# Graph-network kernel: the output pass opens with earlier guards, two tiles made ahead and eight undivided tiles

## The reference, cut to what matters

```python
hp = (node_adj > 0) @ hW              # hW = h @ W[k], per head k
hm = (node_adj < 0) @ hW
e_plus  = leaky_relu(concat([hp, hm], 1) @ a, 0.2)
e_minus = leaky_relu(concat([hm, hp], 1) @ a, 0.2)
att = where(edge_adj > 0, e_plus[None, :], NEG_INF)
att = where(edge_adj < 0, e_minus[None, :], att)
att = softmax(att, axis=1)
edge_support += (att * edge_adj) @ hW     # summed over the 3 heads, then / 3
...
node_output = gru_cell(edge_support, h, node weights)
x = x + de * edge_output + dn * node_output
```

## Time and profile before

| | |
|---|---|
| median of 3 runs | 2030.96 us |
| the profiled execution's own time | 2032.97 us |
| span of its trace (first to last instruction) | 2031.2 us |
| mean granted TensorE clock | 0.978 of full speed |
| PE / DVE / ACT busy | 92% / 74% / 67% of the span |
| sums pass, last part (1239 to 1306 us) | PE busy 66.80 of 67 us |
| output pass, first chunk (1306 to 1399 us) | PE busy 81.00 of 93 us, ACT 89.54 |
| output pass, third chunk's 88 us (1488 to 1576 us) | PE busy 86.13, ACT 77.92 |

### The profile page before, as it was taken

The page is one execution under the profiler, slowest core; times in us unless marked ns, Lnnn a source line. Parts: engine busy times, 40 slices in busy tenths (PEclk is TensorE's granted clock), DMA queues, the critical chain, the costliest instruction groups (busy, mean ns, idle before and its releaser), DMA issues.

```text
span 2031.2 us, 24901 instructions
## 1 busy us (share of the span) xinstructions
PE 1867.2 (92%) x9423; PEld 1309.6 (64%) x9423; DVE 1505.4 (74%) x2278; ACT 1366.1 (67%) x1760; POOL 13.4 (1%) x15
## 2 busy tenths in 40 slices
PE   4877889699988999999999989899999999999998
PEld 4877888488878989955555556544555555554554
DVE  6222226888877888887878753499898898988986
ACT  4222221466668999988777630399898898988984
POOL 0000000000010000000000000000000000000000
PEclk9999999899999999989999999999999999999999
DMA  9999997688866767669999789533343333334230
GB/s 382 424 424 424 424 425 279 238 323 314 318 250 221 270 243 265 249 219 361 354 327 363 265 311 373 178 119 114 114 154 116 114 119 117 132 123 146 99 99 21
DMA packets 88794, 498.12 MB, mean 245 GB/s; under 512 B 9265, under 2 KB 13362, under 8 KB 39266
## 3 DMA queue, kind: packets, MB, share of 16 engines
q1 hardware_dynamic: 84354, 494.34, 65.1%
q10 hardware_dynamic: 4320, 2.20, 0.4%
HBM read 456.55 MB, written 39.94 MB: 244 GB/s over the span
## 4 chain that ended last, share of the span: by engine, by line
PE 52%; DMA 15%; ACT 14%; DVE 14%; issue 5%; SPq 0%; ACTq 0%; DVEq 0%
PE bank L1972 15%; DMA work<-in_adj_rows 12%; PE bank L1946 4%; ACT work L755 4%; PE bank L1785 3%; ACT work L750 3%; PE bank L1787 3%; PE bank L1786 3%; PE bank L1858 2%; DVE work L1581 2%; PE bank L1980 2%; PE bank L1981 2%; ACT work L906 2%; PE bank L1979 2%; PE bank L1863 2%
## 5 line engine op out<-in xcount | busy, mean ns | idle before, releaser
L1972 PE MATMUL bank<-work,reg 128*128 128x512 f32 x760 | 359.2, 597 | 14.6 <-DVE ring L1532 7.9
L906 ACT ACTIVATE work<-x,e 128x512 f32<-128x512 f32 x552 | 355.1, 709 | 0.4 <-ACT linebuf L871 0.4
L1581 DVE TENSOR_TENSOR work<-work,ring 128x1536 f32<-128x1536 f32 x184 | 321.2, 1749 | 9.2 <-ACT work L906 9.0
L1696 PE MATMUL bank<-reg,ring 128*128 128x128 f32 x2048 | 251.0, 284 | 52.3 <-DMA ring<-in_adj_units 29.7
L1696 PEld LDWEIGHTS bank<-reg,ring 128*128 128x128 f32 x2048 | 243.4, 199 | 58.8 <-issue 37.7
L1816 PE MATMUL bank<-reg,ring 128*128 128x129 f32 x2048 | 242.8, 281 | 26.0 <-DVE ring L1275 25.7
L1816 PEld LDWEIGHTS bank<-reg,ring 128*128 128x128 f32 x2048 | 238.2, 197 | 29.9 <-DVE ring L1275 19.1
L1972 PEld LDWEIGHTS bank<-work,reg 128*128 128x128 f32 x760 | 142.6, 190 | 136.2 <-issue 112.0
L1979 PE MATMUL bank<-s_lo,h_hi 128*128 128x512 f32 x240 | 186.0, 775 | 4.9 <-DVE a_lo L1560 3.7
L1275 DVE SCALAR_TENSOR_TENSOR ring<-ring,work 128x2048 f32<-128x2048 f32 x64 | 147.2, 2300 | 39.3 <-ACT work L755 39.2
L1170 DVE TENSOR_TENSOR a_lo<-ring,a_hi 128x2048 fp32r<-128x2048 f32 x64 | 147.5, 2315 | 17.9 <-ACT a_hi L706 17.5
(11 more groups left out here) (295 smaller groups left out, 3073.7 us busy)
## 6 DMA issues: line engine op xcount, KB each, us to landing
ring<-in_adj_units SPq DMA_DIRECT2D x320, 1024.0 KB, 5.5
work<-in_adj_rows SPq DMA_DIRECT2D x38, 1024.0 KB, 22.6
ring<-masks SPq DMA_DIRECT2D x64, 512.0 KB, 5.7
ring<-in_adj_rows SPq DMA_DIRECT2D x26, 1024.0 KB, 22.4
masks<-work SPq DMA_DIRECT2D x48, 512.0 KB, 8.7
masks<-ring SPq DMA_DIRECT2D x16, 512.0 KB, 8.2
x<-lines SPq DMA_DIRECT2D x8, 768.0 KB, 10.4
ring<-lines SPq DMA_DIRECT2D x8, 768.0 KB, 7.9
```

Of the source, the lines that this page charges most:

```text
L906: last = act.activation(tiles(n)[:, k * W:(k + 1) * W], guard(c, k), ACT.Sigmoid, bias=e6[:, t * SCORES + k:t * SCORES + k + 1], scale=-1.0)
L1581: dve.tensor_tensor(tv, tv, spread(ring[:, ring_at("out", g, q * W, W)], HEADS, 1), ALU.mult).then_inc(s_y, 1)
L1696: last = pe.matmul(o, ring[:, first:first + P], reg1[:, t * P:(t + 1) * P], start=t == 0 and i == 0, stop=t == T - 1 and i == Q - 1)
L1972: return pe.matmul(bank[1 + k][:, :], reg1[:, t * P:(t + 1) * P], tiles(c * T + t)[:, k * W:(k + 1) * W], start=t == 0, stop=t == T - 1)
```

## The change

`WHOLE_TILES = 8` is new. The third head of tiles 0 to 7 is no longer divided: ACT makes no high part and DVE no low part for them, and PE multiplies all three heads in plain f32. The places of high parts are counted over the divided tiles alone (`cuts`). `weights(0)` and `weights(1)` move in ACT's list from behind `keep_norm(8)` to between `guards(7)` and `guard_rows(7)`. SP issues the fetch of the first guards before the mask load of unit 44 instead of behind that of unit 63.

```diff
+WHOLE_TILES = 8
...
         CUT = T - 2
+        cuts = [n for n in range(C * T) if n % T < CUT and n >= WHOLE_TILES]
+
+        def is_cut(n):
+
+            return n % T < CUT and n >= WHOLE_TILES
 
         def cut_index(n):
 
-            return (n // T) * CUT + n % T
+            return cuts.index(n)
...
                     sp.dma_start(xs_d, x[:, :]).then_inc(s_xs, 16)
+                if n == 44:
+                    load_guards(0)
                 load_masks(n)
-            load_guards(0)
             load_guards(1)
...
+            for c in range(1, C):
+                keep_norm(c)
+                guards(c)
+                if c == C - 1:
+                    for n in range(AHEAD):
+                        weights(n)
+                guard_rows(c)
+            keep_norm(C)
...
             def third_high(n):
 
                 i = cut_index(n)
                 if i >= PLACES:
-                    act.wait_ge(*tile_used(i - PLACES + 2 * ((i - PLACES) // CUT)))
+                    act.wait_ge(*tile_used(cuts[i - PLACES]))
...
-            for n in range(AHEAD):
-                weights(n)
             for c in range(C):
...
-                    if t < CUT:
+                    if is_cut(n):
                         third_high(n)
...
-                        if 0 < t <= CUT:
+                        if t and is_cut(n - 1):
                             third_low(n - 1)
...
-                            if k == LAST:
+                            if k == LAST and is_cut(c * T + t):
                                 pe.wait_ge(s_ylo, cut_index(c * T + t) + 1)
                                 last = third_tile(c, t)
                             else:
-                                head_tile(c, t, k)
+                                last = head_tile(c, t, k)
```

More of the change, by code:

```diff
@@ L873, in guard_rows @@
                 act.dma_start(lines_d[:, (c - 1) * W:c * W], linebuf[:, :]).then_inc(s_line, 16)
[L875 to L879, removed]
-            def keep_edge_support(c):
-                act.wait_ge(s_es, c)
-                if c > 1:
-                    act.wait_ge(s_gm["out"], c - 1)
-                act.activation(n_temps[0], bank[0][:, :], ACT.Copy, scale=1.0 / HEADS).then_inc(s_src["out"], 1)
-            def store(c):
-                act.wait_ge(s_res["out"], c)
-                act.dma_start(out_d.rearrange("(t p) f -> p t f", p=P)[:, at(c, Q, -Q, Q), :],
-                              res.rearrange("p (t f) -> p t f", f=P)).then_inc(s_store, 16)
             def weights(n):
@@ L908, in weights, with keep_edge_support, store @@
                 last.then_inc(s_exp, 1)
+            for c in range(1, C):
[6 more added lines that the diff above has]
+            keep_norm(C)
+            def keep_edge_support(c):
+                act.wait_ge(s_es, c)
+                if c > 1:
+                    act.wait_ge(s_gm["out"], c - 1)
+                act.activation(n_temps[0], bank[0][:, :], ACT.Copy, scale=1.0 / HEADS).then_inc(s_src["out"], 1)
+            def store(c):
+                act.wait_ge(s_res["out"], c)
+                act.dma_start(out_d.rearrange("(t p) f -> p t f", p=P)[:, at(c, Q, -Q, Q), :],
+                              res.rearrange("p (t f) -> p t f", f=P)).then_inc(s_store, 16)
             def third_high(n):
```

## The result

The changed kernel takes 2022.91 us, the median of 5 runs (2021.48 to 2028.54), against 2031.25 for the kernel before in runs of the same measurement: a ratio of 0.9957, 95% interval 0.9944 to 0.9969. The forecast was 2021.4 us in a range of 2019.2 to 2023.6.

What follows compares the result with a forecast made beforehand. ACT's list was taken to bound the first chunk and PE's pace the later ones. Savings of 4.96 + 4.16 + 0.4 = 9.5 us from 2030.96 gave 2021.4 us, range 2019.2 to 2023.6.

Steps and rivals of the forecast that it cites:

- Which engine sets the first chunk: Output pass: ACT's list ends the first chunk, PE's pace sets later ones; chunk 1 earlier by d saves d.
- Two tiles and the table moved: Behind the copy of the last sums, ACT loses the Sigmoid table load and two tiles: 4.96 us saved.
- The room in the gap: ACT's idle before chunk 7's row copy hides the moved work with 0.1 to 0.9 us in hand.
- The drain: At the moved table load, the skill's extra drain was rejected; it would have meant some 2022 us.
- Eight high parts: First chunk, tiles 0 to 7: eight high parts of 0.52 us leave ACT's list, 4.16 us saved.
- 0.4 off ACT's wait: At tile 8's high part ACT waits 2.5 us for DVE's linked steps in place of 2.97.
- PE's 1.9 us for the plain products: Tiles 0 to 7 cost PE 1.9 us more, covered by about 2 us in hand before chunk 1.
- The guards' fetch: Issued at unit 44 of the sums pass, it costs 0, bounds 0 and 1.1 us lost to late masks.
- TensorE's clock: Slow start at the opening goes, already in the sum; about 2 us idle and slow start stay at chunk 1.
- Only one part arrives: Rival: in the first chunk one of the two main terms is lost, 2026 to 2027 us; chance 0.04.
- The idle at the boundary goes: Rival at chunk 1: slow start gone, 2020.6 to 2020 us, or 2018 without the idle too; chance 0.10.
- plain products alone keep PE slow: Rival in tiles 0 to 7: plain products hold TensorE at 1.2 GHz, about 2042 us; chance 0.02.

Runs made afterwards that it cites:

- e1: Changed kernel with WHOLE_TILES = 0, so only the two tiles, table load and early fetch move; 2026.18 us, opening (sums pass's end to chunk 1) 88.28 us.
- e10: Changed kernel with two more Sigmoids, into columns nothing reads, behind tile 1 in front of chunk 7's row copy; opening 84.90 us against 83.86.
- e8: Changed kernel with table load and tiles 0 and 1 behind chunk 7's row copy instead of ahead of it; opening 90.55 us against 83.86.
- e2: Changed kernel with the two tiles and the guards' fetch back in their old places, leaving eight undivided tiles; 2031.14 us, ratio 0.9997, opening 90.45 us.
- e4: Changed kernel with the first guards' fetch back behind the last mask load; 2023.64 us in one run, opening 83.85 us.
- e3: Kernel before with only the first guards' fetch moved ahead of unit 44's mask load; opening 93.38 us, same as before.
- e5: Changed kernel with WHOLE_TILES = 10 instead of 8; 2016.69 us, ratio 0.9928, opening 80.76 us.
- e6: Changed kernel with DVE's take_chunk one tile earlier, at t == 1 instead of t == 2; 2008.59 us, ratio 0.9890.
- e9: Eight undivided tiles alone (e2), with PE's turn of the last sums behind tile 0 instead of tile 3; opening 88.75 us.

## Why the prediction was right

By the steps of the prediction:

- **Which engine sets the first chunk.** Right, and the base of all else. In e1 PE starts 5.1 us earlier and then idles 4.7 us; the opening shrinks by what ACT's list lost. The last 4.35 us are DVE's list, which follows ACT's; the count is the same from either. From the high part of tile 8 to that of tile 33 I worked out 61.9 and the trace has 61.89, with 2.09 to PE's start for 2.08. The later chunks keep their pace: the rest shrinks by 9.6 where the opening does by 9.52.
- **Two tiles and the table moved, 4.96.** Measured 5.10 (e1). The room in the gap I put at 0.1 to 0.9 us. It is under 0.1: the load starts at 1305.07 and DVE's next instruction at 1305.08, so the add to `s_arg` comes at the late end of its bounds. e10 shows that all beyond is paid, e8 what it costs to miss the gap.
- **The drain.** The Trainium skill ("ScalarE: Activation LUTs", section What ACT_TABLE_LOAD costs) gives about 1380 ns of drain beside the load's 1283. In the moved place the load takes 1.28 and the first Sigmoid starts 0.02 behind it, at 1306.37. A drain ahead of the load could hide in its wait of 1.54 us there; in the kernel before it has no such wait, and it starts 0.02 behind the end of the copy (1306.55 to 1306.57) with no drain to be seen. With a drain behind the load the last sums would have been copied some 1.3 us late, and they are copied 0.03 us behind the pass. Here the measurement decides against it.
- **Eight high parts, 4.16, and 0.4 off ACT's wait.** From e1 to the changed kernel are 4.42 us: 4.16 and 0.26, the wait being 2.71 and not the 2.5 of my working. This holds behind the move; without it the same part brings 2.93 (e2). That the two parts together come to 9.52 as forecast is partly luck: the first is 0.14 above its forecast and the second 0.14 below. PE's 1.9 us for the plain products are covered, as said. That the turn of the last sums is the next thing to be late was right: it ends the wait of DVE's steps at 1322.7 with DVE free since 1322.6.
- **The guards' fetch, 0 of 0 to 1.1.** The cost is right: masks landed 1.3 us later and PE waited 0.2 us at most. The clause beside it, "without it the first part is not to be had", is wrong: e4 has the same opening without it. I had not held the fetch's old landing against the first Sigmoid's start behind the table load. The 8.9 us of rows 9 were misread too: they are the median of the two fetches, which land 8.3 and 9.6 us behind their issues, so they did not land together within 8.9 but in 10.1. With the 9.6 that the one fetch took in e3 the prediction's sum gives an upper bound of 1.8 us and not 1.1.
- **TensorE's clock.** As forecast: full clock in tiles 0 to 7 behind 0.73 us idle; slow records again at chunk 1 behind 2.00 us idle. What they cost was too low in my numbers: I read 0.8 us at least off the first four records, and by the length of chunk 1 (89.08 before, 89.13 after, 87.42 without slow records in e10) it is 1.7. As the cost is the same before and after, the forecast did not suffer.
- **Rivals.** "Only one part arrives" took the two terms as independent, 2026 for either. e2 shows that the second alone brings 2.93 and not 4.2, because the slow start that I booked as harmless ("ACT bounds there") is harmless only while PE's turn of the sums is in time. In the kernel before it is, with divided tiles; with undivided ones it isn't. "The idle at the boundary goes" needed two more undivided tiles (e5) or an earlier take-out (e6). That plain products alone keep PE slow is out: the first 24 take 10.54 us, full clock.

The forecast 2021.4 against 2022.91 measured leaves 1.5 us. The opening gives the forecast's 9.5 and the whole rest 9.6, so the error is not in the change. Of the 1.5 us 0.3 are the kernel before, whose median is 2031.25 in five runs and was 2030.96 in three. The other 1.2 fit into the scatter of the part ahead of the change, which moved by up to 8 us from one execution to the next. Only one of the five runs has a trace, so this is not shown, and what makes that part vary was not tried.

## What to carry to other kernels

Where several engines run at nearly the same pace, find the one whose list has no gaps between two points and count only what leaves or enters that list: here 4.96 and 4.56 us came out to 0.14 each, while 5 us of earlier start on another engine were worth nothing by themselves. Work moved into an idle gap is free up to the gap's length and costs its full time beyond it, so take the gap from the last event that the work waits for, and from nothing earlier. And look at what stands in front of the instruction that frees a buffer: one multiply and one low part too many ahead of `take_chunk` cost more than this whole change brought.

## What the runs showed of the hardware

- Records behind an idle PE are not slow by the length of the idle alone. Behind 2.00 us idle four records of plain f32 took 1.96 us in e10, 2.43 in e8, 2.74 before and 3.57 after; behind 1.78 us idle at e10's opening none was slow, and behind 5.81 us always some were (3.60 and 3.78 for four, 12.04 for 24).
- What a slow stretch costs can't be read off the first records behind the idle. Chunk 1 was 89.08 to 89.13 us long in the six executions in which its first four records took 2.43 to 3.57 us, and 87.42 to 87.45 in the three (e3, e9, e10) in which they took 1.95 or 1.96: about 1.7 us each time, whether the granted clock fell to 0.50 (1.2 GHz) at the first record or, as before the change, a microsecond later.

```profile
1399.30:1400.30 1.00, 1.00 (x3) 0.52 (x4) 1.00 (x3) 1.00 (x3) 0.00 (x0) 1.00 0.00 0
1400.30:1401.30 1.00, 1.00 (x4) 0.49 (x2) 1.00 (x2) 1.00 (x2) 0.00 (x0) 0.52 0.00 0
```

- Twelve kernels that do the same work up to the end of the sums pass, but for the place of one fetch and of six Sigmoids, reached it after 1303.07 to 1310.99 us in one profiled execution each. A change worth 3 us (e2) is out of reach of ten runs' median there and plain in the lengths of one trace.
